# A graph-attention pair stage rebuilt: negated scores, another order of merges and multiplies, operands made earlier

## The chip, the cores and the metric

The kernel runs on one core of a Trainium2 chip. The time is the device time of one execution in microseconds (us), and lower is better. The engines are TensorE (PE in the profile, with PEld for its weight loads), VectorE (DVE), ScalarE (ACT), GpSimd (POOL) and SyncE (SP, which only issues transfers here). They run beside each other and meet at semaphores.

## The reference, cut to what matters

Two layers, each with a graph network, an attention-like mix and a small mixture of experts, on 625 nodes with 512 features and 10,000 edges. The change is in the second layer's graph network, a graph attention with 8 heads of 64, and in products around it:

```python
def _gat_forward(x, edge_index, W_e, W_r, a):          # x: 625 x 512
    h_e = einsum('nf,hfd->hnd', x, W_e)
    h_r = einsum('nf,hfd->hnd', x, W_r)
    a_src, a_dst, a_dif, a_abs, a_prd = split(a, 5, axis=1)
    diff = h_r[:, dst] - h_r[:, src]
    score = (s_src[src] + s_dst[dst] + diff . a_dif
             + |diff| . a_abs + (h_r[:, src] * h_r[:, dst]) . a_prd)
    alpha = leaky_relu(score, 0.2)
    att = softmax of alpha over the edges of one src
    out = segment_sum(att[:, :, None] * h_e[:, dst], src)
```

Beside it stand a linear attention with its projections (`L1_mix`) and, on either side, the two expert stages, whose first products have 512 + 96 columns.

## The kernel before, in words

The score of an edge depends on its two ends alone but for the term in `|diff|`. So the kernel does it in two stages.

**Edge turns** (40 of them, `TURNS`). The 10,000 edges are 80 columns of 125. In each turn two columns get their `|diff|` term: one from rows that GpSimd gathers from a table in HBM (L644, two gathers), one from one-hot products on TensorE (L896, L909). VectorE makes the scores (L1753 to L1767), and GpSimd scatters them, by column, into two tables of pairs in HBM (L654, `pairs[0]` and `pairs[1]`, each 625 x 625 x 8), whose other places hold -1e30. Beside this run the linear attention's products, a few per turn: `KEYS`, `QUERIES`, `VALUES`, `KEYS_TURNED`, `CONTEXT`, `ATTENDED`, `PROJECTED` (L91 to L97) say in which turn which product comes. They share two slots of PSUM.

**Operands.** After the last turn, TensorE turns the eight heads of `hrx` (L974 to L976, `("rT", h)`). ScalarE makes `rhsx` from each (L1266) and VectorE `lhsx` (L1815), after it has finished the small factors `prdx` and `not_last` (L1804 to L1811).

**Pair stage.** Five tiles of 125 source nodes, eight heads each: 40 pairs g = 8 i + h. For a tile, SyncE loads its rows of both tables, the first into one of two buffers `pt`, the second into `stage`, in two halves (L521 to L533). It waits for the buffer's old tile and, for a half of `stage`, for the four merges that read it. For one pair:

- TensorE makes the product of `lhsx` and `rhsx` (L988, by `product`, L694), 625 columns as 512 + 113.
- VectorE adds the table and takes the row's maximum (L1844), takes -0.2 of that (L1850), applies the leaky ReLU (L1851, both inputs the same SBUF tile), and makes the exponent's bias (L1854).
- ScalarE takes the exponential (L1283), GpSimd multiplies by the counts of edges (L674).
- TensorE transposes the result four pairs later (`LAG`; L993), ScalarE copies it (L1277), TensorE multiplies it with `hea` (L1003).
- VectorE merges the next tile's two tables with a maximum, a head's width at a time (L1830): two merges behind each of the heads 4 to 7, and all eight of the first tile before the first pair.
- After heads 3 and 7 of a tile, six pairs late, VectorE divides by the sums, adds to `x` (L1867 to L1875) and takes the statistics of the finished tile (L1310 to L1314), with GpSimd's power behind them (L573).

The slots of PSUM go round in an order written out in `psum_jobs` (L100); pair products and transposes share three. So TensorE's transposes for pair g - 4 take the slot that VectorE empties with L1844 of pair g - 1.

The two expert stages make their first products with the same `product`, 608 columns as 512 + 96 (L865, L1015).

## Time and profile before

| what | us |
|---|---|
| median of 3 runs | 1163.75 (1163.67 to 1176.94) |
| the profiled execution's own time | 1156.31 |
| its span, first to last instruction | 1154.5 |
| edge turns, first gather to last scatter landed | 695.6 to 919 |
| loads and merges of the first tile | 919 to 937.2 |
| pair stage, first L1844 to last L1851 | 937.2 to 1087.3 |
| rest: last sums, transposes, second expert stage, store | 1087.3 to 1154.5 |

The profile is that of one execution. A stretch's row gives the busy time of each engine and the clock that TensorE was granted as a share of full speed: 1.00 is 2.4 GHz and 0.50 is 1.2 GHz, and values between are a mean of the two. A timeline's row gives the start of an instruction (or of a run of like ones), its length, engine, line, operation and operands, and in brackets how long the engine had been idle and for whom. A busy TensorE is not one at its peak, since its matmuls are pipelined.

### The profile page before, as it was taken

What the parts mean: (1) busy time and instruction counts of PE and PEld (TensorE: products, weight loads), DVE (VectorE), ACT (ScalarE), POOL (GpSimd) and SP (SyncE); (2) the same over time, 40 slices, a digit from 0 to 9 for tenths busy, and PEclk for the clock granted to TensorE, in tenths of its full rate; (3) what the DMA queues carried; (4) which work ended last, traced back from release to release, by engine and by line L of the source; (5) the groups of instructions that cost most, each with busy time, mean ns of one, the idle gap of its engine ahead of it and who ended that gap; (6) DMA issues with size and microseconds to landing.
All of it is one profiled execution on the core that took longest, in us unless ns stands there. A gap on an engine that the chain in (4) does not pass through costs nothing.

```text
span 1154.5 us, 11895 instructions
## 1 busy us (share of the span) xinstructions
PE 1017.9 (88%) x4204; PEld 656.2 (57%) x4204; DVE 799.6 (69%) x1363; ACT 320.1 (28%) x561; POOL 361.5 (31%) x321
## 2 busy tenths in 40 slices
PE   7779988999999988999896988999879758888888
PEld 6755488644475445744443436666665436677744
DVE  8994496534587566954435378998988779998732
ACT  5682264311400123022103112221211214333401
POOL 5371700000020102001000117777777514444300
PEclk9889995999999998999897998999989759876999
DMA  9997020021410024001120324333333274442001
GB/s 295 310 310 232 0 100 1 1 90 39 151 37 0 1 90 132 5 0 53 45 109 0 136 49 139 102 98 93 101 95 96 89 311 179 178 176 89 9 1 45
DMA packets 65315, 115.09 MB, mean 100 GB/s; under 512 B 11393, under 2 KB 43393, under 8 KB 63341
## 3 DMA queue, kind: packets, MB, share of 16 engines
q1 hardware_dynamic: 56301, 93.08, 23.7%
q0 software_dynamic: 8960, 21.31, 6.7%
q8 instruction: 32, 0.52, 0.2%
q14 instruction: 22, 0.18, 0.0%
HBM read 85.88 MB, written 28.49 MB: 99 GB/s over the span
## 4 chain that ended last, share of the span: by engine, by line
PE 49%; DVE 24%; POOL 11%; issue 8%; DMA 6%; ACT 1%; DVEq 0%; POOLq 0%; SPq 0%
PE ps L699 25%; PE ps L826 8%; POOL arena L644 6%; DMA pairs<-arena,pairi 5%; PE ps L724 4%; PE ps L691 4%; DVE arena L1500 4%; POOL pairs L654 3%; DVE arena L1844 3%; DVE arena L1851 3%; PE ps L1003 2%; PE ps L876 2%; PE ps L1027 2%; PE ps L762 2%; DVE arena L1830 1%
## 5 line engine op out<-in xcount | busy, mean ns | idle before, releaser
L699 PE MATMUL ps<-arena 128*125 128x512 f32 (+4 forms) x576 | 250.4, 584 | 14.7 <-DVE small L1844 7.9
L699 PEld LDWEIGHTS ps<-arena 128*125 128x125 f32 (+2 forms) x576 | 112.5, 205 | 135.0 <-issue 121.5
L573 POOL TENSOR_TENSOR small<-small 125x1 f32<-125x1 f32 x50 | 33.0, 660 | 440.6 <-DVE small L1314 440.6
L699 PE MATMUL ps<-arena,xnT 128*125 128x512 f32 (+1 forms) x440 | 166.3, 536 | 1.6 <-DVE x L1743 1.6
L691 PE MATMUL ps<-ident,arena 125*128 125x125 f32 (+3 forms) x545 | 89.6, 310 | 57.3 <-DVE small L1844 17.9
L699 PEld LDWEIGHTS ps<-arena,xnT 128*125 128x125 f32 x440 | 76.5, 189 | 84.5 <-issue 83.7
L691 PEld LDWEIGHTS ps<-ident,arena 125*128 125x128 f32 (+3 forms) x545 | 74.8, 182 | 79.4 <-issue 30.5
L909 PE MATMUL ps<-ex_low,high 125*125 125x512 f32 x400 | 107.3, 416 | 0.0
L1185 ACT ACTIVATE arena<-ps,cols 128x125 f32<-128x125 f32 x120 | 43.2, 466 | 213.4 <-PE ps L691 213.4
L654 POOL DMA_INDIRECT pairs<-arena,pairi x80 | 87.6, 1095 | 26.1 <-issue 25.0
L674 POOL TENSOR_TENSOR arena<-arena,counts 125x625 f32<-125x625 f32 x40 | 62.7, 1567 | 102.5 <-ACT arena L1283 102.5
L909 PEld LDWEIGHTS ps<-ex_low,high 125*125 125x125 f32 x400 | 74.2, 194 | 16.7 <-issue 0.5
L724 PE MATMUL ps<-arena 125*125 125x314 f16 x400 | 66.6, 332 | 16.6 <-DVE arena L1357 15.6
L1039 ACT ACTIVATE arena<-ps 125x625 f32<-125x625 f32 (+4 forms) x79 | 49.3, 647 | 105.1 <-PE ps L691 102.1
L724 PEld LDWEIGHTS ps<-arena 125*125 125x125 f16 x400 | 59.9, 154 | 23.2 <-DVE arena L1357 18.8
L826 PE MATMUL ps<-arena 128*125 128x512 f32 x160 | 70.5, 593 | 1.7 <-DVE arena L1505 1.7
L1561 DVE TENSOR_TENSOR x<-x,ps 125x512 f32<-125x512 f32 x30 | 20.5, 685 | 61.1 <-PE ps L699 25.6
L1283 ACT ACTIVATE arena<-arena,small 125x625 f32<-125x625 f32 x40 | 32.7, 817 | 100.6 <-DVE small L1854 100.6
L1003 PE MATMUL ps<-arena 125*125 125x96 f32 x400 | 59.9, 307 | 0.0
L1003 PEld LDWEIGHTS ps<-arena 125*125 125x125 f32 x400 | 57.8, 226 | 0.0
L1767 DVE TENSOR_REDUCE arena<-arena 125x8 f32<-125x512 f32 x80 | 54.6, 683 | 2.2 <-DMA pairs<-arena,pairi 0.8
L1844 DVE CUSTOM_DVE_ANT_0 arena<-ps,arena 125x625 f32<-125x625 f32 x40 | 51.5, 1287 | 4.9 <-PE ps L699 4.8
(211 smaller groups left out, 1594.3 us busy)
## 6 DMA issues: line engine op xcount, KB each, us to landing
pairs<-fill SPq DMA_DIRECT2D x10, 2500.0 KB, 22.0
arena<-pairs SPq DMA_DIRECT2D x5, 2500.0 KB, 9.5
arena<-pairs SPq DMA_DIRECT2D x10, 1250.0 KB, 12.3
arena<-in_mw SPq DMA_DIRECT2D x6, 2048.0 KB, 8.3
arena<-in_rows SPq DMA_DIRECT2D x16, 250.0 KB
arena<-in_qkv_w SPq DMA_DIRECT2D x1, 3072.0 KB
arena<-in_cw SPq DMA_DIRECT2D x3, 1024.0 KB, 5.3
arena<-in_w_qkvT SPq DMA_DIRECT2D x1, 3072.0 KB
```

What stands on the lines that cost most here:

```text
L644: pool.indirect_dma_start(out=rows[:, g % GATHERS, :], out_offset=None, in_=table, in_offset=bass.IndirectOffsetOnAxis(ap=ends[:, 2 * g:2 ...
L654: pool.indirect_dma_start(out=pairs[n], out_offset=bass.IndirectOffsetOnAxis(ap=pairi[:, t:t + 1], axis=0), in_=sc[:, t % SCORES, :], in_o ...
L674: pool.tensor_tensor(S[:, h, :], S[:, h, :], counts[:, i, 0:N].bitcast(F32), ALU.mult).then_inc(sig("pair_weighted"), 1)
L691: last = pe.transpose(slot[0:n, at:at + rows], src, ident[0:rows, 0:rows])
L699: last = mm(slot[0:m, lo:hi], lhsT_of(k), rhs_of(k)[:, lo:hi], start=(k == 0), stop=(k == ks - 1))
L724: last = mm(ps[0:P, 512 * i:512 * i + HALF], one_hot[:, k, 0, P * i:P * (i + 1)], one_hot[:, k, 1, 0:HALF], start=False, stop=False, skip_ ...
L826: last = mm(slot[0:P, lo:lo + 512], nodes(hT, i)(k), w1[:, k, lo:lo + 512], start=(k == 0), stop=(k == KC - 1))
L909: last = mm(product_at[0:P, at:at + D], hotsT[e % 2][:, i, :], part[:, i, :], start=(part is hr_high and i == 0), stop=(part is hr_low and ...
L1003: last = mm(sums[0:P, at:at + WIDE], exTh[:, h, P * k:P * (k + 1)], hea[:, v0:v0 + WIDE], start=(k == 0), stop=(k == NT - 1), skip_group_c ...
L1039: return act.activation(dst, src, ACT.Copy)
L1767: v.tensor_reduce(sc[0:P, t % SCORES, :], src.rearrange("p (h e) -> p h e", h=H), AX_X, ALU.add)\
L1844: ring.emptied(v.tensor_tensor_reduce(S[:, h, :], slot[0:P, 0:N], p3[:, :, h], 1.0, -3e38, ALU.add, ALU.max, smax[:, 0, h:h + 1]), ("pair" ...
```

## The change

- **Negated scores.** L1844's operation takes the scale -1 and a minimum, so `S` holds negated scores. The bias is then one instruction, `min(0.2 low, low)`, and the leaky ReLU another, also with a minimum; L1850 is gone, and the bias comes first. The exponential has the scale -1.
- **Merge by head.** One merge behind every pair of the first four tiles, where there were two behind each of the heads 4 to 7.
- **Three table buffers.** `pt` has three, at 14300, 19300 and 5000. SyncE waits for the buffer of tile i - 3. The third overlaps `wo1` and the bias `b1or`, so its first load waits for the last `("y1", i)`. `S` keeps six pairs (`SCORED`) and `exTh` three (`TURNED`), where both kept eight.
- **GpSimd's multiply timed.** The multiply of pair g waits, beside the exponential, for the merge behind pair g + 1; in the last tile, for L1851 of pair g + 1.
- **Operands in the edge turns.** The turns of `hrx` come in turns 32 to 39, one head each, and ScalarE makes both `rhsx` and `lhsx`. `prdx` and `not_last` are made before the first edge turn. `PROJECTED` becomes turns 34, 36, 38 and two more behind the last, and the first tile's loads wait for `("oT", 3)` and no longer for `("y1", 4)`.
- **Halved products.** `halves_product` cuts 625 or 608 columns in the middle, across two banks of PSUM, for keys and queries, `oT`, the pair products and both expert stages.

```diff
-    jobs += [(("rT", h), "dve") for h in range(H)]
+    for e in range(PROJECTED[-1] + 1):
...
-        pt = [view(14300 + DT * n, DT) for n in range(2)]
+        pt = [view(at, DT) for at in (14300, 19300, 5000)]
...
-            ring.wait_emptied(sp, ("y1", NT - 1))
+            ring.wait_emptied(sp, ("oT", KC - 1))
             for i in range(NT):
-                if i >= 2:
-                    ring.wait_emptied(sp, ("pair", i - 2, H - 1))
+                if i == 2:
+                    ring.wait_emptied(sp, ("y1", NT - 1))
+                if i >= 3:
+                    ring.wait_emptied(sp, ("pair", i - 3, H - 1))
...
                     pool.wait_ge(sig("pair_exp"), g + 1)
-                    pool.tensor_tensor(S[:, h, :], S[:, h, :], counts[:, i, 0:N].bitcast(F32),
+                    if (g + 1) // H + 1 < NT:
+                        pool.wait_ge(sig("merged"), H + g + 2)
+                    elif g + 1 < NT * H:
+                        pool.wait_ge(sig("bias_ready"), g + 2)
+                    Sg = S[:, g % SCORED, :]
+                    pool.tensor_tensor(Sg, Sg, counts[:, i, 0:N].bitcast(F32),
                                        ALU.mult).then_inc(sig("pair_weighted"), 1)
...
+            def halves_product(slot, m, lhsT_of, rhs_of, ks, n):
+                at, cut = across_banks(n).start, n // 2
+                for lo, hi in ((0, cut), (cut, n)):
+                    for k in range(ks):
+                        last = mm(slot[0:m, at + lo:at + hi], lhsT_of(k), rhs_of(k)[:, lo:hi],
+                                  start=(k == 0), stop=(k == ks - 1))
+                return last
...
+            def rows_turned(h):
+                slot = ring.wait_filled(act, ("rT", h))
+                rows = slot[0:HX, 0:128 * NT].rearrange("p (i n) -> p i n", i=NT)[:, :, 0:P]
+                act.activation(rhsx[:, h, :].rearrange("p (i n) -> p i n", i=NT), rows,
+                               ACT.Identity, scale=not_last, bias=ident[0:HX, HX - 1:HX])
+                ring.emptied(act.activation(lhsx[:, h, :].rearrange("p (i n) -> p i n", i=NT),
+                                            rows, ACT.Identity, scale=prdx_of(0, h),
+                                            bias=prdx_of(1, h)), ("rT", h))
...
                     ring.emptied(v.tensor_tensor_reduce(
-                        S[:, h, :], slot[0:P, 0:N], p3[:, :, h], 1.0, -3e38, ALU.add, ALU.max,
-                        smax[:, 0, h:h + 1]), ("pair", i, h))
+                        Sg, slot[0:P, across_banks(N)], p3[:, :, h], -1.0, 3e38, ALU.add,
+                        ALU.min, smax[:, 0, h:h + 1]), ("pair", i, h))
...
-                    st.did(TS(smax[:, 2, h:h + 1], smax[:, 0, h:h + 1], -0.2, None, ALU.mult))
-                    st.did(STT(out=S[:, h, :], in0=S[:, h, :], scalar=0.2, in1=S[:, h, :],
-                               op0=ALU.mult, op1=ALU.max))
-                    st.wait()
-                    STT(out=smax[:, 1, h:h + 1], in0=smax[:, 0, h:h + 1], scalar=-1.0,
-                        in1=smax[:, 2, h:h + 1], op0=ALU.mult, op1=ALU.min)\
+                    low = smax[:, 0, h:h + 1]
+                    STT(out=smax[:, 1, h:h + 1], in0=low, scalar=0.2, in1=low, op0=ALU.mult,
+                        op1=ALU.min)
+                    STT(out=Sg, in0=Sg, scalar=0.2, in1=Sg, op0=ALU.mult, op1=ALU.min)\
                         .then_inc(sig("bias_ready"), 1)
-                    if i + 1 < NT and h >= 4:
-                        merge(i + 1, 2 * (h - 4))
-                        merge(i + 1, 2 * (h - 4) + 1)
+                    if i + 1 < NT:
+                        merge(i + 1, h)
```

## Rows read from the trace of the kernel before

**Rows 1.** Stretches: length, busy (count) PE, PEld, DVE, ACT, POOL; clock, DMA share, GB/s.

```profile
695.60:919.00 223.40, 201.04 (x911) 137.77 (x912) 193.65 (x316) 46.58 (x70) 172.11 (x160) 0.94 0.35 96
937.20:1087.50 150.30, 128.41 (x685) 102.61 (x686) 141.42 (x280) 53.53 (x75) 63.55 (x43) 0.78 0.36 142
```

**Rows 2.** Waits of GpSimd in the edge turns: us in total, times, longest.

```profile
POOL pairs L654 <- issue: 25.0, 79, 0.6
```

**Rows 3.** Groups by line in the pair stage: busy us, mean ns, idle before.

```profile
L674 POOL TENSOR_TENSOR arena<-arena,counts 125x625 f32<-125x625 f32 x39 | 61.4, 1574 | 100.7 <-ACT arena L1283 100.7
...
L1844 DVE CUSTOM_DVE_ANT_0 arena<-ps,arena 125x625 f32<-125x625 f32 x40 | 51.5, 1287 | 4.9 <-PE ps L699 4.8
L1851 DVE SCALAR_TENSOR_TENSOR arena<-arena 125x625 f32<-125x625 f32 x40 | 43.6, 1089 | 0.0
...
L1830 DVE TENSOR_TENSOR arena<-arena 125x625 f32<-125x625 f32 x33 | 25.2, 803 | 0.0
...
L1850 DVE TENSOR_SCALAR small<-small 125x1 f32<-125x1 f32 x40 | 6.1, 154 | 1.4
L1875 DVE TENSOR_TENSOR x<-x,arena 125x256 f32<-125x256 f32 x8 | 4.7, 591 | 0.3
```

**Rows 4.** Timeline (start, length) of one pair in which the two engines meet.

```profile
1006.65 1.29 POOL L674 TENSOR_TENSOR arena<-arena,counts 125x625 f32<-125x625 f32 x1 [1.87 <-ACT arena L1283]
...
1007.09 1.52 DVE L1851 SCALAR_TENSOR_TENSOR arena<-arena 125x625 f32<-125x625 f32 x1
```

**Rows 5.** Timeline of a pair with two merges ahead of it.

```profile
994.36 1.52 DVE L1830 TENSOR_TENSOR arena<-arena 125x625 f32<-125x625 f32 x2
...
995.37 1.66 POOL L674 TENSOR_TENSOR arena<-arena,counts 125x625 f32<-125x625 f32 x1 [2.08 <-ACT arena L1283]
995.91 1.30 DVE L1844 CUSTOM_DVE_ANT_0 arena<-ps,arena 125x625 f32<-125x625 f32 x1
...
997.33 0.80 DVE L1851 SCALAR_TENSOR_TENSOR arena<-arena 125x625 f32<-125x625 f32 x1
...
998.16 0.16 DVE L1854 SCALAR_TENSOR_TENSOR small<-small 125x1 f32<-125x1 f32 x1
```

**Rows 6.** Timeline, TensorE: transposes after a tile's end, and two later products.

```profile
989.73 1.38 PE L691 MATMUL ps<-ident,arena 125*125 125x125 f32 x5 [3.62 <-DVE small L1844]
...
995.12 1.28 PE L691 MATMUL ps<-ident,arena 125*125 125x125 f32 x5
...
1001.09 1.26 PE L699 MATMUL ps<-arena 66*125 66x512 f32 x4
...
1003.81 1.26 PE L699 MATMUL ps<-arena 66*125 66x512 f32 x4
```

**Rows 7.** Stretches of 5 us around that tile's end; columns as in rows 1.

```profile
985.00:990.00 5.00, 1.38 (x6) 0.75 (x5) 4.76 (x12) 0.55 (x1) 2.44 (x2) 0.83 0.00 0
990.00:995.00 5.00, 5.00 (x19) 3.96 (x19) 4.90 (x10) 1.93 (x3) 1.67 (x1) 0.50 0.22 54
```

**Rows 8.** Timeline: the queue of the loads, and the first merges.

```profile
919.09 18.42 SPq L440 DMA_DIRECT2D arena<-pairs  x6
...
931.25 5.90 DVE L1830 TENSOR_TENSOR arena<-arena 125x625 f32<-125x625 f32 x8 [5.79 <-DMA arena<-pairs]
```

**Rows 9.** Stretch of 5 us behind the second tile's loads.

```profile
945.00:950.00 5.00, 3.05 (x7) 1.45 (x6) 4.90 (x8) 1.55 (x3) 1.58 (x2) 0.50 0.01 4
```

**Rows 10.** Timeline: the first gather; first and last of the operands' small steps.

```profile
695.65 1.57 POOL L644 DMA_INDIRECT arena<-table,srci  x1 [5.73 <-DVEq L1713]
...
911.49 0.15 DVE L1805 TENSOR_TENSOR prdx<-prdx 64x8 f32<-64x8 f32 x1
...
912.20 0.15 DVE L1809 TENSOR_SCALAR small<-ident 66x1 f32<-66x1 f32 x1
```

**Rows 11.** Chain that ended last: the first products of the two expert stages.

```profile
588.05 21.52 PE ps L699 x80
...
1099.05 21.52 PE ps L699 x80
```

152 lines of the change are left out of this document (79 added, 73 removed).

## The prediction, before the changed kernel was seen

> **What bounds the kernel now.** I read the stretches first, to split the span. In the edge turns, 223 us, GpSimd is busy 172 us with 160 instructions [rows 1]. That is not full, but the view of its waits shows what fills the rest: before its scatters it stands 25.0 us in 79 pieces in which it waits for nothing, 0.3 us each [rows 2]. So the turns run at the pace at which GpSimd issues. VectorE (194 us) and TensorE have some room there. The pair stage, 150.3 us, is another matter: VectorE is busy 141.4 us, 94% of it, and TensorE has a mean clock of 0.78 [rows 1]. Between the two lie loads: they are issued at 919.09, the first merge waits for them until 931.25, and the eight merges take to 937.2 [rows 8].
>
> The groups by line then say what VectorE does in the pair stage [rows 3]: 40 each of L1844 at 1.29 us and L1851 at 1.09 us, the merges at 0.80, and small steps. The odd one is L1851. The timeline shows it at 0.80 us where it runs alone [rows 5], and at 1.52 us where GpSimd's multiply has begun 0.44 us ahead of it [rows 4]. The multiply then takes 1.29 us; where a merge is running as it begins, it takes 1.66 us [rows 5]. The one that comes second waits. L1844, which has one input in PSUM, is not lengthened by a multiply beside it (1.30 us in [rows 5], its mean is 1.29).
>
> **The change, part by part.** The sum goes by the profiled execution (1156.31 us, of which 1154.5 are its span). The median of three runs is 7.4 us longer, and I carry that difference over unchanged.
>
> *The timed multiply.* It now begins as the merge of the next pair ends, beside L1844 of the pair after that. L1851 begins 1.42 us after L1844 (995.91 to 997.33, [rows 5]) and the multiply alone takes 1.29 [rows 4], so it fits if it starts within 0.13 us. Then all L1851 take 0.80: 40 x (1.09 - 0.80) = -11.6 us [rows 3, 5]. Bounds: 0 (it slips and they meet again) and -11.6; No row shows how soon the release reaches GpSimd; I take -11.6, and the slip is a rival of its own below. The multiply comes later than now, but the transposes that need it come four pairs later and, as now, wait for a slot of L1844 three pairs on, so this stays hidden by some 3 us.
>
> The Trainium skill (SBUF — State Buffer, Who interferes with whom) says that VectorE and GpSimd share a pair of ports as an exclusive lock: an operation of VectorE with two SBUF inputs and a GpSimd operation that reads SBUF do not overlap, and the later one blocks to the end of the first. The trace agrees (1.52 against 0.80). By that rule the multiply does not vanish but meets other work, and this speaks against a part of the gain.
>
> That other work is L1875, which adds to `x` from two SBUF tiles behind the merge in two steps of each tile. Its mean is 0.59 us over 8 [rows 3]. Where the multiply starts just ahead of it, it could lose up to 0.4 each; between 0 and 3.2 I take +1.6 us.
>
> *Negated scores.* L1850 goes: 40 x 0.154 = 6.1 us busy [rows 3]. How much of it ran beside its neighbours no row tells, so the gain lies between 0 and 6.1; I take half, -3.1 us. The bias is ready after L1851 as before.
>
> *Merge by head.* The count of merges is the same and so is their price, 0.78 (two in 1.55, [rows 5]). What moves is the first need: the second tile's first merge comes 2.25 us (1.42 + 0.83, [rows 5]) behind 937.2, not after four pairs. Its half of `stage` is not there. The loads of two tiles, in the order of the queue, end at about 945: in the 5 us behind, the transfers are idle [rows 9]. From 919.1 to 945 that is 26 us for four equal pieces, 6.5 each, so the last half (3.2 us) begins near 942. VectorE waits from 939.5 to 942 or, with the landing, 943: +2.5 to 3.5, I take +3 us. From then on a step is 1.42 + 0.83 + 0.78 = 3.03 us, and the third buffer brings each tile's first table a tile earlier, so no later load is late.
>
> *TensorE as the next bound.* At full clock it needs 2.72 us for a pair (1001.09 to 1003.81, [rows 6]), at half clock 5.39 (989.73 to 995.12). The full clock suffices for 3.03, not for the last tile, which has no merges: 2.25 against 2.72 there, 7 steps, up to +3.3; part of that is given back in the blocks of sums, where VectorE is the later one. I take +2.5 us.
>
> At half clock TensorE is the bound of any step. After a tile's sums it stands idle 3.62 us [rows 6], its clock falls from full to half (0.83 as a mean of 5 us, then 0.50, [rows 7]), and VectorE pays: L1844 waits 4.8 us for products over the whole stage [rows 3]. With steps of 3.03 instead of twice that with two merges in every second half, a half-clock pair costs more (5.39 against 3.03). The idle gap itself gets some 0.8 us shorter, one merge less. Between no stalls (-4.8) and 29 us (below) I take +2 us, nearer to now because the pause that starts it is still there.
>
> *Operands in the edge turns.* The block between 911 and 925 vanishes, but it ran beside the last scatters and the loads, which set the merges' start [rows 8]; nothing is gained by it. In turns 34 to 38 TensorE had a projection in every turn and now has one in every second, with the turned rows beside. ScalarE takes on two operations a head, with 46.6 us busy of 223 [rows 1]. Both stay behind GpSimd's issue; if that cover were gone, eight turned heads would cost some 0.7 us each, 5.5 in all (five transposes take 1.38 at half clock, [rows 6]). The two late projections run while the loads do; the third buffer waits for them, and it is issued only after six others. But the small factors are now made ahead of the first gather, which waits for VectorE [rows 10]: from 911.49 to 912.35, 0.86 us. GpSimd's 160 instructions shift with it: +0.9 us.
>
> *Halved products.* Five products of 608 columns take 21.52 us in each expert stage, and that is the chain that ended last [rows 11], 4.30 each. The eight passes of 96 columns are the ones too short to cover a weight load. If one of 304 covers it no better, nothing is gained. At full clock a product is 16 passes of 304 columns at two cycles a column (an estimate: the pair products' 625 columns in four passes fit in their 1.26 us, [rows 6]), 16 x 0.253 = 4.05. So up to -0.25 each, 10 of them: 0 to -2.5, I take -2.1 us. In the pair stage and the turns it is hidden.
>
> **Sum.** -11.6 + 1.6 - 3.1 + 3 + 2.5 + 2 + 0.9 - 2.1 = -6.8 us, 1149.5 on the profiled execution's count. Against the median, 1163.75 - 6.8 = **1157 us**.
>
> **Rivals.** *The full gain.* The steadier rhythm keeps the clock up: TensorE's 2.72 of 3.03 leaves it 0.3 us of idle a step, where a step with two merges (1.42 + 0.83 + 1.55 = 3.80) left over 1. Then the 4.8 us of stalls go too (instead of +2), the last tile gives 2.5 less, and L1875 loses nothing: -6.8 - 6.8 - 2.5 - 1.6 = -17.7, **1146 us**. For it: in an even stretch the pairs ran at full clock [rows 6]. Against: the pause behind each tile remains. The Trainium skill (TensorE: Matmul & The Clock Gate, Part 1: The HAM clock gate) says that half rate is the default and activity lifts it; by that rule fewer and shorter pauses would bring this rival's time, and the trace shows both levels.
>
> *The multiply misses its window.* Only 0.13 us of margin; a later start of 0.3 us on every pair lets L1851 wait again. The 11.6 us stay: -6.8 + 11.6 = +4.8, **1168.6 us**. For it: the two engines start on semaphores of different ages. Against: two waits that have both long been met but one.
>
> *TensorE's low clock takes the stage* (the other side). A mean clock of 0.78 [rows 1] is 44% of 150 us at half rate, 66 us. If those all bind, each of the 12 pairs in them takes 5.39 and not 3.03: 12 x 2.36 = 29 us, 27 more than I put in: **1184 us**. It decides against the change from about four such pairs beyond mine (6.8 / 2.36 = 2.9). Against: a TensorE that is the bound is never idle, and after the fall at 990 with no idle time in 5 us [rows 7] its pairs were back at 2.72 by 1001 [rows 6].
>
> *Nothing moves:* gains and new waits cancel, 1160 to 1166. It is the forecast's upper part.
>
> **How the numbers follow.** Forecast, with its neighbours 1150 to 1165: 0.55. Full gain, 1143 to 1150: 0.18. Missed window, 1165 to 1171: 0.15. Low clock, over 1171: 0.10. Other: 0.02. The range 1146 to 1171 leaves out the low clock's case and the end of the full gain, about 2 in 10. Over 2%, about what a measurement of this kernel can tell from no change, is 23 us: faster would need 1140, which no sum here reaches (0.05); slower needs 1187, the end of the low clock's case (0.05). Within 2%: 0.90.
>
> **What would show it.** In the profile after: L1851 with a mean near 0.80 us (right) or over 1.0 (missed window); the multiply near 1.3 us, not 1.57; one wait of L1830 for a load near 943; the first L1844 at about 938; L1844's waits for TensorE near 7 us; 20.3 us for five expert products. The forecast fails if L1851 stays long, or if the clock of the pair stage leaves 0.78 by much in either direction.

## The result, and the profile after

| | before | after |
|---|---|---|
| median of 20 runs each, us | 1165.24 (1156.36 to 1176.94) | 1158.63 (1149.24 to 1166.44) |
| profiled execution, its span | 1156.31, 1154.5 | 1153.63, 1151.5 |
| pair stage, first add to last leaky ReLU | 937.18 to 1087.30 = 150.12 | 937.61 to 1083.86 = 146.25 |
| VectorE busy in it | 141.27 | 131.06 |

The ratio after to before is 0.9945, 95% interval 0.9923 to 0.9967: 6.4 us faster, where 6.8 were forecast (1157 us). The size is right. Much of the way to it is not, and the experiments show that more was left lying than was gained.

In the changed kernel the add with its row's extreme is L1873 (it was L1844), the bias L1880 (L1854), the leaky ReLU L1882 (L1851), the merge L1858 (L1830), the addition to `x` L1901 (L1875), GpSimd's multiply L692 (L674), the pair product L726. VectorE's groups by line in the pair stage (busy us, mean ns, idle before and its releaser), which answer [rows 3]:

```profile
L1873 DVE CUSTOM_DVE_ANT_0 arena<-ps,arena 125x625 f32<-125x625 f32 x40 | 51.5, 1288 | 8.4 <-PE ps L726 8.1
L1882 DVE SCALAR_TENSOR_TENSOR arena<-arena 125x625 f32<-125x625 f32 x40 | 32.0, 800 | 0.0
L1858 DVE TENSOR_TENSOR arena<-arena 125x625 f32<-125x625 f32 x32 | 25.6, 800 | 4.2 <-DMA arena<-pairs 4.2
L1880 DVE SCALAR_TENSOR_TENSOR small<-small 125x1 f32<-125x1 f32 x40 | 9.8, 244 | 1.4
L1901 DVE TENSOR_TENSOR x<-x,arena 125x256 f32<-125x256 f32 x8 | 8.6, 1077 | 0.3
```

The leaky ReLU is at 0.80 in every pair, as forecast. But the bias, an instruction of one column, went from 0.159 to 0.244, and the addition to `x` from 0.591 to 1.077 on average. The bias in the kernel before:

```profile
L1854 DVE SCALAR_TENSOR_TENSOR small<-small 125x1 f32<-125x1 f32 x39 | 6.2, 159 | 1.3
```

The timeline of VectorE and then of GpSimd shows the pair in which this happens (start, length):

```profile
946.80 0.80 DVE L1858 TENSOR_TENSOR arena<-arena 125x625 f32<-125x625 f32 x1
947.52 1.30 DVE L1873 CUSTOM_DVE_ANT_0 arena<-ps,arena 125x625 f32<-125x625 f32 x1
948.74 0.08 DVE L1873 DVE_READ_ACCUMULATOR2_ANT small<- 125x1 f32 x1
948.86 0.41 DVE L1880 SCALAR_TENSOR_TENSOR small<-small 125x1 f32<-125x1 f32 x1
949.19 0.80 DVE L1882 SCALAR_TENSOR_TENSOR arena<-arena 125x625 f32<-125x625 f32 x1
```

```profile
947.75 1.50 POOL L692 TENSOR_TENSOR arena<-arena,counts 125x625 f32<-125x625 f32 x1 [29.14 <-ACT arena L1317]
```

The multiply starts 0.22 us after the add (947.75 against 947.52), not within 0.13, and takes 1.50, not 1.29. It ends at 949.25. The bias begins at 948.86, reads two SBUF operands (the same column twice), and lasts until the multiply is over. The leaky ReLU behind it is free again.

The other half of the picture is TensorE's clock. Stretches of the changed kernel, columns as in [rows 1], first the whole stage, then three pieces around the sums of the second tile's first half:

```profile
937.61:1083.86 146.25, 123.98 (x682) 102.75 (x683) 131.06 (x239) 54.38 (x75) 59.51 (x42) 0.80 0.38 147
970.00:975.00 5.00, 3.47 (x22) 2.42 (x20) 4.86 (x10) 1.39 (x2) 2.12 (x2) 1.00 1.06 454
975.00:980.00 5.00, 4.66 (x19) 4.13 (x20) 4.64 (x10) 2.21 (x3) 1.43 (x2) 0.59 0.32 131
980.00:985.00 5.00, 5.00 (x29) 4.50 (x29) 3.50 (x6) 1.67 (x3) 2.72 (x2) 0.73 0.76 256
```

TensorE stands idle for 1.87 us up to 975.34, its clock falls from 1.00 to 0.59, and in the 5 us behind it TensorE is busy throughout while VectorE works 3.50 of 5. Outside the stage, the five products of an expert stage are the rows of the chain of work that ended last, which answer [rows 11]:

```profile
589.35 20.48 PE ps L726 x80
...
1096.20 20.48 PE ps L726 x80
```

### The profile page after: what moved, and what is told of

Its sections match the earlier page's. It is cut to its first block, busy times and chain, and to the rows that moved or that the text cites. A ratio compares the mean times of both kernels' runs of the same rounds, so it can differ in the third digit from the quotient of the medians.

```text
span 1151.5 us, 11896 instructions
## 1 busy us (share of the span) xinstructions
PE 1009.2 (88%) x4204; PEld 667.0 (58%) x4204; DVE 781.3 (68%) x1315; ACT 325.8 (28%) x569; POOL 358.7 (31%) x321
## 4 chain that ended last, share of the span: by engine, by line
PE 50%; DVE 23%; POOL 11%; issue 8%; DMA 7%; ACT 0%; DVEq 0%; SPq 0%; POOLq 0%
PE ps L717 21%; PE ps L853 8%; POOL arena L657 6%; PE ps L726 5%; DMA pairs<-arena,pairi 5%; PE ps L709 4%; DVE arena L1534 4%; POOL pairs L667 4%; DVE arena L1873 3%; PE ps L751 2%; PE ps L1029 2%; DMA arena<-pairs 2%; PE ps L903 2%; PE ps L1054 2%; PE ps L789 2%
## 5 line engine op out<-in xcount | busy, mean ns | idle before, releaser
L717 PE MATMUL ps<-arena 128*125 128x512 f32 x400 | 180.2, 606 | 0.0
L586 POOL TENSOR_TENSOR small<-small 125x1 f32<-125x1 f32 x50 | 35.5, 710 | 435.5 <-DVE small L1348 435.5
L709 PE MATMUL ps<-ident,arena 125*128 125x125 f32 (+3 forms) x545 | 85.2, 298 | 51.1 <-DVE small L1873 14.2
L717 PE MATMUL ps<-arena,xnT 128*125 128x512 f32 x280 | 126.0, 608 | 4.2 <-DVE x L1786 4.2
L717 PEld LDWEIGHTS ps<-arena 128*125 128x125 f32 x400 | 75.2, 193 | 89.9 <-issue 89.9
L667 POOL DMA_INDIRECT pairs<-arena,pairi x80 | 87.2, 1090 | 25.5 <-issue 25.5
L717 PEld LDWEIGHTS ps<-arena,xnT 128*125 128x125 f32 x280 | 53.6, 194 | 69.7 <-issue 69.3
L692 POOL TENSOR_TENSOR arena<-arena,counts 125x625 f32<-125x625 f32 x40 | 58.0, 1452 | 105.7 <-ACT arena L1317 92.0
L726 PE MATMUL ps<-arena 66*125 66x313 f32 (+3 forms) x176 | 65.1, 500 | 24.6 <-DVE small L1873 16.3
L853 PE MATMUL ps<-arena 128*125 128x512 f32 x160 | 70.5, 593 | 1.7 <-DVE arena L1539 1.7
L1595 DVE TENSOR_TENSOR x<-x,ps 125x512 f32<-125x512 f32 x30 | 20.5, 684 | 62.1 <-PE ps L717 25.4
L1873 DVE CUSTOM_DVE_ANT_0 arena<-ps,arena 125x625 f32<-125x625 f32 x40 | 51.5, 1288 | 8.4 <-PE ps L726 8.1
L726 PEld LDWEIGHTS ps<-arena 66*125 66x125 f32 (+1 forms) x176 | 35.3, 220 | 36.7 <-DVE small L1873 18.0
```

Source lines behind the costliest of these rows:

```text
L667: pool.indirect_dma_start(out=pairs[n], out_offset=bass.IndirectOffsetOnAxis(ap=pairi[:, t:t + 1], axis=0), in_=sc[:, t % SCORES, :], in_o ...
L692: pool.tensor_tensor(Sg, Sg, counts[:, i, 0:N].bitcast(F32), ALU.mult).then_inc(sig("pair_weighted"), 1)
L709: last = pe.transpose(slot[0:n, at:at + rows], src, ident[0:rows, 0:rows])
L717: last = mm(slot[0:m, lo:hi], lhsT_of(k), rhs_of(k)[:, lo:hi], start=(k == 0), stop=(k == ks - 1))
L726: last = mm(slot[0:m, at + lo:at + hi], lhsT_of(k), rhs_of(k)[:, lo:hi], start=(k == 0), stop=(k == ks - 1))
L853: last = mm(slot[0:P, lo:lo + 512], nodes(hT, i)(k), w1[:, k, lo:lo + 512], start=(k == 0), stop=(k == KC - 1))
```

## The experiments

The kernel before ran beside each on the same chip, and the ratio is to those runs. "Stage" is the profiled stretch from the first add to the last leaky ReLU.

| kernel | median us | ratio to before, 95% interval | stage | VectorE busy in it | adds' wait for TensorE | merges' wait for the load |
|---|---|---|---|---|---|---|
| before | 1165.24 | 1 | 150.12 | 141.27 | 4.8 | 0 |
| changed | 1158.63 | 0.9945 (0.9923 to 0.9967) | 146.25 | 131.06 | 8.1 | 4.2 |
| 1 no timed wait | 1161.04 | 0.9937 (0.9899 to 0.9975) | 151.52 | 134.61 | 9.9 | 4.3 |
| 2 released by `bias_ready` | 1154.88 | 0.9917 (0.9883 to 0.9952) | 144.18 | 128.38 | 8.8 | 4.3 |
| 3 operands late | 1160.74 | 0.9977 (0.9929 to 1.0025) | 150.15 | 130.54 | 12.9 | 3.9 |
| 4 before, timed multiply alone | 1156.41 | 0.9912 (0.9871 to 0.9953) | 153.87 | 136.40 | 13.4 | 0 |
| 5 gaps filled | 1150.75 | 0.9883 (0.9797 to 0.9969) | 143.01 | 131.12 | 4.8 | 4.1 |
| 6 merges later | 1154.93 | 0.9938 (0.9884 to 0.9991) | 143.14 | 130.63 | 9.5 | 0 |
| 7 no timed wait, bias of one tensor | 1159.74, one run | none | 154.23 | 133.98 | 13.3 | 4.2 |
| 8 = 2 + 5 + 6, and filled ahead, too late | 1164.16 | 0.9998 (0.9952 to 1.0044) | 160.47 | 131.42 | 26.2 | 0 |
| 9 = 5 + 6, more filling | 1148.26 | 0.9862 (0.9814 to 0.9910) | 137.57 | 131.10 | 3.7 | 0 |
| 10 = 9, filled ahead too | 1145.73 | 0.9843 (0.9799 to 0.9887) | 135.90 | 131.28 | 1.9 | 0 |
| 11 = 10 + 2 | 1152.28 | 0.9871 (0.9822 to 0.9919) | 150.49 | 132.43 | 15.0 | 0.3 |
| 12 = 10, `x` added from PSUM, fewer filling products | 1141.11 | 0.9807 (0.9778 to 0.9837) | 131.69 | 126.39 | 2.7 | 0 |

A profiled stage is one execution, and the adds' waits for TensorE differ by 5 us between kernels whose pair stage is the same (8.1 and 12.9 in the changed kernel and in 3). So I read an edit's worth from VectorE's busy time and from the wait it is about, and the whole from the intervals. None of the runs 1 to 6 is parted from the changed kernel by its interval; 9 to 12 are.

### 1. The timed wait left out

```diff
-                    if (g + 1) // H + 1 < NT:
-                        pool.wait_ge(sig("merged"), H + g + 2)
-                    elif g + 1 < NT * H:
-                        pool.wait_ge(sig("bias_ready"), g + 2)
```

> The changed kernel with GpSimd's timed wait left out: the multiply again starts as soon as its exponential is there. My theory, that the time of the start is what keeps the multiply off the leaky ReLU: L1878 (the leaky ReLU, 0.80 in the changed kernel) goes to 1.0 to 1.5 us in the steps where they meet, L1858's merges stay near 0.80, and the stage from the first add to the last leaky ReLU goes from 146.25 to 152 to 158 us, the time up by 6 to 11 us. Rival, that one merge to a head instead of two in every other head separates them by itself: the leaky ReLU stays under 0.9 us on average and the time moves by under 2 us.

Measured, VectorE's groups in the stage (L1878 is this kernel's leaky ReLU, L1876 its bias):

```profile
L1878 DVE SCALAR_TENSOR_TENSOR arena<-arena 125x625 f32<-125x625 f32 x40 | 32.0, 800 | 0.0
...
L1876 DVE SCALAR_TENSOR_TENSOR small<-small 125x1 f32<-125x1 f32 x40 | 14.5, 362 | 1.4
```

My theory falls in its main point: without the wait the leaky ReLU is at 0.80 in all 40 pairs. It is not the time of the multiply that keeps it free. The change also put the bias ahead of the leaky ReLU, and now the bias is the first instruction that meets the multiply: 0.16 where it is alone, up to 1.22 where it is held up, 14.5 us in all. What the timed wait is worth in this kernel is the bias's 14.5 - 9.8 = 4.7 us, or 3.5 us of VectorE's busy time (134.61 - 131.06), not 11.6. The rival is half right: the leaky ReLU stays under 0.9, and in this kernel the bias ahead of it takes the block. The stage, 151.52, was just short of what I expected, and 1.8 us of it are waits for TensorE (9.9 against 8.1); by time the two kernels can't be told apart.

### 7. The same with a bias that reads one tensor

```diff
-                    STT(out=smax[:, 1, h:h + 1], in0=low, scalar=0.2, in1=low, op0=ALU.mult,
-                        op1=ALU.min)
+                    TS(smax[:, 1, h:h + 1], low, 0.2, low, ALU.mult, ALU.min)
```

> The changed kernel without the timed wait, and with the small bias instruction written as one that reads a single tensor from SBUF (its factor and its second term come as the instruction's scalars). Without the wait and with the two-tensor form the bias took 0.362 us on average and the leaky ReLU 0.80. My theory, that the multiply blocks whichever two-tensor SBUF instruction comes first while it runs: the bias comes back to 0.15 to 0.17 and the leaky ReLU behind it takes the block, 0.95 to 1.05 on average. Rival, that every small SBUF instruction is slowed by the multiply: the bias stays above 0.30 and the leaky ReLU at 0.80.

Measured: the view of one line gives least, median and largest length in ns, for the bias and for the leaky ReLU.

```profile
L1876 DVE TENSOR_SCALAR small<-small x40: 211/214/216, 938.2 to 1089.5; 125x1 f32<-125x1 f32 x40
```

```profile
L1877 DVE SCALAR_TENSOR_TENSOR arena<-arena x40: 799/801/1707, 938.4 to 1089.7; 125x625 f32<-125x625 f32 x40
```

This settles it for the two instructions. A bias that reads one tensor has the same length in every pair, 0.21, with the multiply beside it (21 of the 40) or not; and the block goes to the next instruction with two SBUF tensors, the leaky ReLU, which is longer than 0.85 in 15 of the 40 pairs and has a mean of 0.920. I had put the bias at 0.15 to 0.17 (this form is simply longer than the other, 0.21 against 0.16) and the leaky ReLU's mean a little higher. There is one execution of this kernel, so its time says nothing.

### 4. The timed multiply alone, in the kernel before

```diff
+                    i1, h1 = divmod(g + 1, H)
+                    if i1 + 1 < NT and h1 >= 4:
+                        pool.wait_ge(sig("merged"), H * (i1 + 1) + 2 * (h1 - 4) + 2)
+                    elif i1 < NT:
+                        pool.wait_ge(sig("bias_ready"), g + 2)
                     pool.tensor_tensor(S[:, h, :], S[:, h, :], counts[:, i, 0:N].bitcast(F32),
```

> The kernel before with one part of the change alone: its multiply waits for the next step's merges, or where there are none for the next step's bias. My theory, that the timed start is the largest part: the leaky ReLU L1851 goes from a mean of 1.09 to 0.80 to 0.85, 10 to 11.6 us of VectorE's time, of which the two small instructions before it (0.15 and 0.16) may give back up to 0.5 us each in the half of the steps without merges, so that the time falls by 2 to 10 us. Rival, that without the merges spread over all heads no start is free: where a step has no merges the multiply still meets the leaky ReLU, its mean stays above 0.95, and the time falls by under 2 us or rises.

Measured in its stage (L1849 the add, L1856 the leaky ReLU, L1880 the addition to `x`):

```profile
L1849 DVE CUSTOM_DVE_ANT_0 arena<-ps,arena 125x625 f32<-125x625 f32 x40 | 51.6, 1291 | 13.5 <-PE ps L704 13.4
L1856 DVE SCALAR_TENSOR_TENSOR arena<-arena 125x625 f32<-125x625 f32 x40 | 33.8, 846 | 0.0
...
L1880 DVE TENSOR_TENSOR x<-x,arena 125x256 f32<-125x256 f32 x8 | 9.2, 1156 | 0.3
```

In the old order the timed wait does what the prediction said: the leaky ReLU goes from 43.6 to 33.8 us. Of these 9.8 us, 4.5 come back in the addition to `x` (4.7 to 9.2). The time falls by 0.5 to 1.3%, as much as with the whole rebuilt stage. The profiled execution itself was not a good one (1163.92 us): a stage of 153.87 with 13.4 us of waits for TensorE.

### 2. The multiply released by `bias_ready`

```diff
-                    if (g + 1) // H + 1 < NT:
-                        pool.wait_ge(sig("merged"), H + g + 2)
-                    elif g + 1 < NT * H:
+                    if g + 1 < NT * H:
                         pool.wait_ge(sig("bias_ready"), g + 2)
```

> The changed kernel with the multiply's wait for the next head's merge replaced by one for that head's bias everywhere: it is issued while the merge runs and should start where the merge ends, without a semaphore's way from VectorE (in the changed kernel it starts 0.22 us after the add). My theory, that its end at 1.5 to 1.7 us after the add is what lengthens the small bias instruction from 0.16 to 0.41: the bias instruction comes back to 0.16 to 0.20, VectorE's busy time in the stage falls from 131 to 123 to 127 us, and the stage from 146.25 to 140 to 144 us, less than VectorE's gain, since TensorE needs 2.72 us for a pair. Rival, that the bias instruction is longer for another reason (its two operands): it stays at 0.24 on average and nothing moves. A second rival: the multiply gets in ahead of the merge, whose mean then goes from 0.80 to over 1.2, and the stage is longer by 5 us or more.

The semaphore `bias_ready` is raised by the leaky ReLU, since the bias now comes ahead of it. So the multiply is released as the next head's leaky ReLU ends, about where the merge begins.

Measured (L1878 is the bias, L1880 the leaky ReLU, L1856 the merge, L1354 the normalised `x`), the groups and then one place in the timelines of VectorE and of GpSimd:

```profile
L1856 DVE TENSOR_TENSOR arena<-arena 125x625 f32<-125x625 f32 x32 | 25.7, 804 | 4.3 <-DMA arena<-pairs 4.3
...
L1878 DVE SCALAR_TENSOR_TENSOR small<-small 125x1 f32<-125x1 f32 x40 | 6.6, 166 | 1.4
L1354 DVE TENSOR_SCALAR xn<-x,small 125x512 f32<-125x512 f32 x3 | 3.8, 1265 | 0.0
```

```profile
1000.57 0.81 DVE L1856 TENSOR_TENSOR arena<-arena 125x625 f32<-125x625 f32 x1
1001.29 1.52 DVE L1354 TENSOR_SCALAR xn<-x,small 125x512 f32<-125x512 f32 x1
```

```profile
1000.80 1.73 POOL L690 TENSOR_TENSOR arena<-arena,counts 125x625 f32<-125x625 f32 x1 [1.56 <-DVE arena L1880]
```

My theory holds in its cause: the bias is back at 0.166, and the merges are not delayed. In size it fell short: VectorE loses 2.7 us of work (131.06 to 128.38, not to 127 or less), and the stage, 144.18, is just outside 140 to 144. The multiply is issued while the merge runs, and its record is longer for it (most are 1.71 to 1.96 us), but it is over 1.44 us after the add began (952.60 against 951.16), where the changed kernel's was over after 1.73 (949.25 against 947.52). The bias, which begins 1.34 us after the add in both, meets only the last 0.1 us of it. That the multiply waits for the merge's end and starts then is my reading of the lengths. The bias gives 3.2 us and the addition to `x` 1.7 (8.6 to 6.9), and the normalised `x` takes 2.2 back: its three take 1.52, 1.74 and 0.54 us in place of 0.54 each; the two long ones begin behind a multiply's start, the short one ahead of it (1060.08 against 1060.31). It reads one SBUF tensor only, so it is not the number of tensors alone that decides who is blocked. The gain in the stage, 2.1 us, is below what two profiles of one kernel differ by.

### 3. The operands turned late again

```diff
-ROWS_TURNED = (32, 33, 34, 35, 36, 37, 38, 39)
+ROWS_TURNED = (40, 41, 42, 43, 44, 45, 46, 47)
```

with the three loops over turns carried on to turn 47.

> The changed kernel with its eight operand turns put behind the last edge turns again (as in the kernel before, though ScalarE still makes both operands). My theory, that the loads of the first tile's tables set the start of the pair stage and the place of the operands is hidden: the first add starts within 0.5 us of where it did (937.61), the time moves by under 1.5 us. Rival, that the move gained something: the first add starts 2 us or more later against the first load's issue, and the time goes up by as much.

Measured: the first load is issued at 922.4 and the first add begins at 940.47, 18.1 us later; in the changed kernel 919.8 and 937.61, 17.8; before 919.09 and 937.18, 18.1. VectorE's busy time in the stage is the same (130.54). So the move of the operands is hidden, as forecast. The first add is 2.9 us later against the span's beginning: 0.9 of that is there at the first gather (698.04 against 697.17), 1.7 arise in the turns, which have less to do here, and 0.3 behind them; the stage is longer by waits for TensorE. None of this can be put down to the moved work. The medians (1160.74 and 1158.63) don't part.

### 5. TensorE's gaps filled

```diff
+                if i < NT and g % 4 == 3 and g >= 11:
+                    bank = 0 if g % 8 == 7 else 512
+                    for _ in range(12 if g % 8 == 7 else 4):
+                        mm(ring.psum[3][0:P, bank + HW:bank + 512], lhsx[:, h, 0:P], rhsx[:, h, 0:128],
+                           start=False, stop=False, skip_group_check=True)
```

The columns that these products write are read by nothing.

> The changed kernel with products whose result nobody reads (125x128, into unused columns of PSUM) put behind the pair product before TensorE's two gaps of each tile: 4 in the shorter gap (0.96 to 1.87 us in the changed kernel), 12 in the longer one (2.15 to 3.06 us). Nothing else moves. My theory, that the granted clock falls to 0.5 after these gaps and that the add's waits for TensorE (8.1 us in the changed kernel, 8.8 to 13.4 us in the runs around it, the same work each time) come from that: the granted clock stays at 1.0 from the second tile on, the add's wait for TensorE falls to 1 to 3 us, VectorE's busy time stays at 131, and the stage falls from 146.25 to 138 to 142 us. Rival, that TensorE's work of 2.72 us a pair is itself what the add waits for: the wait stays at 7 us or grows by the 3.5 us of work a tile that is added, and the stage is 146 us or longer.

Measured, stretches of this kernel (the stage, one gap with 4 products, one with 12), and then the changed kernel's at the gap with 12.

```profile
939.01:1082.02 143.01, 129.76 (x815) 110.80 (x816) 131.12 (x239) 53.92 (x75) 59.54 (x42) 0.87 0.39 150
970.00:975.00 5.00, 5.00 (x35) 4.14 (x35) 4.86 (x10) 2.47 (x4) 2.81 (x2) 1.00 1.03 442
975.00:980.00 5.00, 4.01 (x22) 3.67 (x21) 4.93 (x10) 1.39 (x2) 1.29 (x1) 0.69 0.55 235
980.00:985.00 5.00, 5.00 (x20) 4.43 (x19) 3.83 (x7) 2.32 (x3) 1.51 (x1) 0.50 0.61 204
...
1020.00:1025.00 5.00, 4.54 (x36) 4.08 (x36) 4.76 (x13) 0.71 (x2) 1.29 (x1) 1.00 0.00 0
1025.00:1030.00 5.00, 5.00 (x34) 3.84 (x32) 4.92 (x9) 2.79 (x4) 3.65 (x3) 1.00 0.15 24
```

```profile
1020.00:1025.00 5.00, 2.85 (x17) 2.58 (x18) 4.86 (x11) 1.39 (x2) 1.22 (x1) 0.87 0.00 0
1025.00:1030.00 5.00, 5.00 (x20) 4.37 (x19) 4.93 (x9) 2.33 (x3) 2.95 (x4) 0.50 0.46 148
```

VectorE has the same work (131.12), TensorE has more, and the stage is 3.2 us shorter. At 1020 to 1030, where the changed kernel's clock fell to 0.87 and 0.50, it stays at 1.00. It still fell behind the first gap, where 4 products left 0.99 us of idle time, and at 1035 to 1045 (0.83 and 0.82) around another gap with 4, which left 0.95. By time the four executions (1149.78 to 1152.19) are not parted from the changed kernel's twenty (1149.24 to 1166.44), but by the clock they are: its mean over a whole execution is 0.927 to 0.931 here and 0.907 to 0.922 there. The adds' wait went from 8.1 to 4.8, not to 1 to 3, and the stage stopped 1 us above what I had expected. The Trainium skill (TensorE: Matmul & The Clock Gate, Part 1: The HAM clock gate) says that the clock is at half rate by default and is lifted and held by activity. The trace agrees: with more work in the gaps the clock of the stage is 0.87 in place of 0.80.

### 6. The second tile's merges later

```diff
-                        merge(i + 1, h)
+                        for k in (MERGED_AT[h] if i == 0 else (h,)):
+                            merge(i + 1, k)
```

with `MERGED_AT = ((), (), (0,), (1,), (2,), (3,), (4, 5), (6, 7))`, and the multiply's wait counted to match.

> The changed kernel with the merges of the second tile put later among the first tile's heads (none at heads 0 and 1, one at 2 to 5, two at 6 and 7), since the second tile's load lands only 6 us after the first add. My theory, that the wait of 4.2 us for that load is the whole price of starting to merge at the first head: the wait goes to 0 to 0.5 us and the stage is shorter by 2 to 4 us, less than 4.2, because TensorE at half clock then sets the first tile's steps. Rival, that TensorE's clock takes all of it back: the add's wait for TensorE grows by 3 us or more and the stage stays within 1 us of 146.25.

Measured (L1878 the add, L1863 the merge):

```profile
L1878 DVE CUSTOM_DVE_ANT_0 arena<-ps,arena 125x625 f32<-125x625 f32 x40 | 51.5, 1287 | 9.9 <-PE ps L731 9.5
...
L1863 DVE TENSOR_TENSOR arena<-arena 125x625 f32<-125x625 f32 x32 | 25.5, 801 | 0.0
```

The load's wait is gone, as the theory said. The wait for TensorE is 1.4 us longer (9.5 against 8.1) and the stage 3.1 us shorter, both as expected, but from one execution each: between two executions this wait differs by more.

### 8 to 11. The parts together

Runs 9 and 10: the merges of 6 and the products of 5, now 8 in place of 4 in the shorter gap; 10 has 34 more behind the third pair product, while the first tables are loaded:

```diff
+                if g == 2:
+                    for _ in range(34):
+                        mm(ring.psum[3][0:P, 384:512], lhsx[:, h, 0:P], rhsx[:, h, 0:128],
+                           start=False, stop=False, skip_group_check=True)
```

> The changed kernel with the later merges of the second tile and the gap products, of which there are now 8 in place of 4 in the shorter gap, since in the run with 4 the clock fell once more behind that gap (0.69 and 0.50 from 975 to 990). My theory, that the two causes add: the load's wait goes (4.2 us), the add's wait for TensorE falls to 2 to 4 us behind the first tile and to 2 to 3 us in it, and the stage from 143.0 and 143.1 us with either alone to 137 to 140 us, the time to 1145 to 1149 us. Rival, that the low clock of the first tile takes back what the later merges give: the stage stays at 142 us or longer.

> As the run before it, with 34 more products behind the third pair product, in the 10 us in which TensorE waits for the first tables (in the earlier try they stood behind the fourth, which waits itself for the first add, and so ran into the first steps at half clock: 26.2 us of waits for TensorE). My theory, that the first tile's half clock comes from that wait: the granted clock is 1.0 from the first step on, the add's wait for TensorE is under 3 us in all, the stage 134 to 138 us, the time 1143 to 1147 us. Rival, that the clock falls all the same in the first tile, whose steps leave TensorE idle until the first sums: nothing is gained over the run before it.

Measured, stretches of 9 and then of 10 (the stage, the first tile's end, the rest):

```profile
943.25:1080.82 137.57, 129.85 (x847) 108.58 (x848) 131.10 (x239) 53.24 (x75) 59.54 (x42) 0.92 0.41 156
...
960.00:965.00 5.00, 5.00 (x21) 4.44 (x20) 3.62 (x6) 1.51 (x2) 1.57 (x2) 0.57 0.74 256
965.00:1080.00 115.00, 110.75 (x785) 94.41 (x784) 110.57 (x204) 45.67 (x65) 51.26 (x36) 1.00 0.34 125
```

```profile
930.00:935.00 5.00, 5.00 (x48) 5.00 (x47) 2.74 (x4) 0.00 (x0) 0.00 (x0) 1.00 1.06 447
940.00:945.00 5.00, 4.47 (x8) 2.32 (x8) 4.89 (x11) 1.63 (x2) 1.35 (x1) 0.50 1.00 414
...
960.00:1075.00 115.00, 109.67 (x776) 93.24 (x776) 110.93 (x205) 44.86 (x64) 51.92 (x37) 1.00 0.34 126
```

With both gaps filled the granted clock is 1.00 over 115 us, and the two edits together give more than the sum of their parts: the stage is 8.7 us shorter than the changed kernel's, where 3.2 and 3.1 came from either alone. My reading is that run 5's 4 products in the shorter gap were too few; the number of products alone was not tried. By time, 9 is 0.9 to 1.9% below before, and clear of the changed kernel (0.9814 to 0.9910 against 0.9923 to 0.9967). Filling ahead (10) lifts the clock to 1.00 at 930 to 935, but it is at 0.50 again when the first pairs run: TensorE stands idle 3.9 us up to 940.53. On the clock the rival is right; the wait fell from 3.7 to 1.9 all the same, and whether the 1.7 us of the stage are more than chance stays open (the intervals overlap).

Run 8 had 36 of these products behind the fourth pair product, which waits for the first add, together with the edits of 2, 5 and 6.

> The changed kernel with the multiply released by the next head's bias everywhere (as in the second run), the second tile's merges put later, the products that fill TensorE's gaps, and 36 more of them ahead of the first step, while the first tables are loaded. My theory, that what is left over the steps of 2.72 us is the bias held up (3 us), the load (4.2) and the low clock (8): VectorE's busy time in the stage is 126 to 129 us, its waits for TensorE and the load under 6 us together, the stage 130 to 137 us, and the time 1142 to 1150 us. Rival, that TensorE's own work becomes the bound as soon as VectorE's steps are shorter: the waits for TensorE come back to 8 us or more and the stage is 138 us or longer.

Its timeline of TensorE shows what became of them:

```profile
937.39 2.45 PE L725 MATMUL ps<-arena 66*125 66x312 f32 x4 [10.40 <-DVE small L1881]
939.63 15.57 PE L1022 MATMUL ps<-arena 66*125 66x128 f32 x72
```

They ran in the first steps instead of ahead of them, at half clock, 15.57 us, and held the pair products up. That is my error in placing them. The merges are longer too (28.2 us against 25.5 in run 6), from the cause that run 11 shows.

Run 11 is 10 with the release of 2.

> As the run before it, with the multiply released by the next head's bias everywhere, so that it starts with the merge's end. My theory, that VectorE's steps get shorter by the 0.08 us on average that the small bias instruction loses (3 us in the stage), and that TensorE's 2.72 us take at least half of that back: the stage is shorter by 0 to 1.5 us. Rival, that the multiply gets in ahead of merges now and then (one merge took 2.1 us in the earlier run of all three): the stage is longer by 1 us or more.

In the profiled execution the stage is longer by 14.6 us, and the rival names the place. That execution, 1158.32 us, is a long one; the medians differ by 6.6 us, and the intervals overlap. Where the first tile has two merges behind one another, the multiply gets in between them. The timelines of VectorE and of GpSimd (L1866 the merge, L691 the multiply):

```profile
965.02 2.84 DVE L1866 TENSOR_TENSOR arena<-arena 125x625 f32<-125x625 f32 x2
```

```profile
965.25 1.94 POOL L691 TENSOR_TENSOR arena<-arena,counts 125x625 f32<-125x625 f32 x1 [2.93 <-DVE arena L1890]
```

Two merges that take 1.52 without it [rows 5] took 2.84. TensorE stood idle 2.05 us up to 969.31, the clock was at 0.56 and then 0.50 from 970 to 990, and the adds' waits rose from 1.9 to 15.0 us. The merges are longer by 4.0 us in all (29.4 against 25.4); the other 13.1 us are waits for TensorE. That these follow from the pause and the clock is likely by the order in time, and not shown by a run of its own. Releasing the multiply by the merges in those two heads alone was not tried.

### 12. The addition to `x` from PSUM

```diff
-                    TT(o.rearrange("p (h e) -> p h e", h=4), s4[:, :, 0:HD],
-                       r.unsqueeze(2).to_broadcast([P, 4, HD]), ALU.mult)\
-                        .then_inc(sig("sums_used"), 1)
-                    v.wait_ge(sig("sums_used"), 2 * j + b + 1)
-                    st.did(TT(x[:, j, 256 * b:256 * (b + 1)], x[:, j, 256 * b:256 * (b + 1)], o,
-                              ALU.add))
+                    for q in range(4):
+                        xq = x[:, j, 256 * b + HD * q:256 * b + HD * (q + 1)]
+                        last = STT(out=xq, in0=s4[:, q, 0:HD], scalar=r[:, q:q + 1], in1=xq,
+                                   op0=ALU.mult, op1=ALU.add)
```

> The kernel with the later merges, the gap products (here 5 and 9 in the two gaps, which get shorter) and the 34 products ahead, with the addition to x written otherwise: four instructions that read one quarter of the sums from PSUM, scale it and add x, in place of a scaling to SBUF (0.424 us) and an addition of two SBUF tensors (0.591 us on average in the kernel before, 1.075 in the run without this edit, eight of each). My theory, that the addition is long because it is blocked by the multiply, and that an instruction with one SBUF tensor is not: four instructions of 0.10 to 0.20 us each, 0.4 to 0.8 us in place of 1.50, so that VectorE's busy time in the stage falls by 5 to 8 us from 131.28 and the stage from 135.9 to 130 to 133 us. Rival, that the quarters cost as much as they save or are blocked as well (over 0.3 us each): the stage stays at 135 us or longer. A second rival, that TensorE is the bound by now: VectorE's busy time falls by 5 us or more, its waits for TensorE rise from 1.9 to 5 us or more, and the stage stays above 134 us.

The products in the gaps are fewer than in 10 as well (5 and 9 in place of 8 and 12), so the time is that of both edits; VectorE's busy time is that of the one shown.

Measured: one line's least, median and largest length in ns, then the stage.

```profile
L1914 DVE SCALAR_TENSOR_TENSOR x<-ps,small,x x40: 274/275/285, 972.1 to 1080.3; 125x64 f32<-125x64 f32 x40
```

```profile
940.19:1071.88 131.69, 123.77 (x794) 102.61 (x795) 126.39 (x255) 53.49 (x75) 59.65 (x42) 0.92 0.42 161
```

This instruction, with one of its two tensors in PSUM, has one length, 0.275, beside the multiply or not; each was longer than I had put it, but four in a row take 0.86 (at 985.38) in place of 0.424 + 1.075. VectorE loses 4.9 us of work, just short of the 5 to 8 expected, the stage 4.2 us, waits for TensorE stay small (2.7). This is the fastest of the kernels: 1141.11 us, 1.6 to 2.2% below before and, by ratio to before, 1.4% below the changed kernel (0.9807 / 0.9945).

## Why the prediction was right, step by step

The sum came to -6.8 us and the measurement to -6.4. Its terms, against the two profiled executions:

| term | forecast | measured | from |
|---|---|---|---|
| leaky ReLU to 0.80 | -11.6 | -11.6 | 43.6 to 32.0 |
| (not in the sum) bias held up | 0 | +3.4 | 40 x (0.244 - 0.159) |
| addition to `x` meets the multiply | +1.6 (0 to 3.2) | +3.9 | 4.7 to 8.6 |
| L1850 gone | -3.1 (-6.1 to 0) | -6.1 | whole of its 6.1 |
| second tile's load late | +3 (2.5 to 3.5) | +4.2 | wait at 943.97 |
| TensorE as the bound, low clock | +4.5 | +3.3 | waits 4.8 to 8.1 |
| small factors ahead of the first gather | +0.9 | +1.3 | below |
| halved expert products | -2.1 | -2.1 | 2 x (21.52 - 20.48) |

**The timed multiply: right in size, wrong in cause.** I took all 11.6 us as the wait's work and wrote that the bias follows the leaky ReLU "as before". The diff puts the bias first, and with two SBUF operands it became the instruction that the multiply blocks. Run 1 shows the leaky ReLU free without the wait, run 7 shows that of the bias and the leaky ReLU the first with two SBUF tensors is blocked, run 4 that the wait alone is worth 9.8 us of the leaky ReLU in the old order. Without the wait the meeting costs 8.1 us at the bias (run 1, 40 x (0.362 - 0.159)) or 4.8 us at the leaky ReLU (run 7, 40 x (0.920 - 0.800)), where it cost 11.6 before. So part of the 11.6 went with the rest of the new order, and which edit took it no run shows. The gap of 1.42 us into which the multiply should fit is there (947.52 to 948.86 is 1.34), the start and the length were underrated: 0.22 and 1.50 us. The rival of the missed window had the lateness nearly right (0.3 us on every pair) and the victim wrong: the price is 0.085 us on the mean bias, up to 0.27 where they meet, not the 11.6 us of the leaky ReLU.

The Trainium skill (SBUF — State Buffer, Who interferes with whom), from which the prediction took the block, also says that an instruction of VectorE with at most one SBUF input, outside the modes in which it uses both ports, does not contend. For the small instructions the trace agrees on both sides: 0.21 and 0.275 us in all 40 places with one SBUF tensor (runs 7 and 12), 0.16 to 0.43 with two in the changed kernel. The condition on the modes matters: the normalised `x`, with one SBUF tensor and 512 columns, took 1.52 and 1.74 us where the multiply had begun before it, and 0.54 where it began first (run 2); that it ran in such a mode no trace shows. The prediction applied the rule to the long instructions alone, and it holds for one of a single column.

**The addition to `x`: undersized.** I worked from its mean of 0.591, and that mean mixed two things: in the trace of before, five of the eight take 0.42 and three 0.87. After, three take 0.94 and five 1.15 or 1.16. So each can lose 0.73, not 0.4, and all eight lose something, where I counted on half. In run 4, which times the multiply in the old order, all eight take 1.15 to 1.17: a multiply that always starts behind a merge always stands ahead of this instruction.

**L1850: undersized.** Half of its 6.1 us was a hedge between 0 and all; all of it went from VectorE's busy time. With it went 1.3 us of idle time: the two small instructions before had 1.4 and 1.3 us ahead of them in all, the one after has 1.4.

**Load, TensorE and clock.** The wait came at 943.97 (I wrote near 943) and took 4.2 us; in run 6 the stage is 3.1 us shorter without it. The waits for TensorE are 8.1 us where I wrote near 7. But the range of this term was the thing to look at: in six kernels with the pair stage of the changed one or nearly so (the changed one, 1, 2, 3, 6, 7) the same wait was 8.1 to 13.3 us. Filling the gaps brought it to 4.8 (run 5), with the later merges to 3.7 (9) and with the filling ahead to 1.9 (10). I had named the pause behind each tile as its start and left it there as given.

**Operands, first gather, halves.** Run 3 shows the operands' move hidden. The first gather is at 697.17 instead of 695.65, 1.52 later; 1.30 of that is there at the first expert stage already (589.35 against 588.05), ahead of everything that was changed, and 0.22 are left. With the 1.04 us that the halved products save in between, the shift to set against the forecast's 0.9 is about 1.3 (0.53 of it the small factors' own stretch, 694.75 to 695.28; where the rest is from I did not follow). The halves are right to 0.1 us. Behind the stage 0.6 us were lost (12.34 from the last leaky ReLU to the second expert stage, against 11.75).

**The sum.** The terms as measured make -3.7 us, and the two profiled executions differ by 2.7 (1156.31 and 1153.63), the medians by 6.6. Stretch by stretch the two spans differ by +1.3 us ahead of the first expert stage, -1.0 in it, +1.3 from there to the first gather, -0.8 in the edge turns, -0.3 from the first load to the first add, -3.9 in the pair stage, +0.6 behind it, -1.0 in the second expert stage and +0.9 after that, -3.0 in all. The sum had a term for four of these nine; the other five, which it put at nothing, moved by 0.3 to 1.3 us, and no run shows why. The profiled execution of before was also a lucky one: it is as short as the shortest of the twenty (1156.36). The mechanisms were mostly the right ones, but that -6.8 met -6.4 so closely is in part luck: three terms were off by 2.3 to 3.4 us with both signs, and one profiled execution stands for the median only to within the waits for TensorE. In the changed kernel the five executions with a mean clock under 0.915 took 1162.0 to 1166.4 us, the eight with 0.918 or more 1149.2 to 1159.2. The full gain of 1146 us, which I gave 0.18 as an accident of the rhythm, is about what runs 9 and 10 reach on purpose (1148.3 and 1145.7 us), by way of the clock and the load and without the part in the addition to `x`, which still loses 3.9 us there.

## What to carry to other kernels

Before a wait is used to move one engine's work out of another's way, list the instructions behind it by what they read, the small ones too: here the block went to the first of them with two SBUF tensors, and an operand left in PSUM (run 12) or a form that reads one tensor (run 7) took a small instruction out of the list. A long one with a single SBUF tensor was blocked all the same (the normalised `x` in run 2). Where a profile shows the granted clock falling behind a regular pause of TensorE, fill the pause before anything else is trimmed: work that nobody reads made this stage shorter, and where TensorE kept its clock a trimmed VectorE showed nearly in full (run 12: 4.9 us of work, 4.2 of the stage). And judge each edit by the busy time and the wait that it touches, since the waits for the clock differ from one execution to the next by as much as a whole edit is worth.

## What was not expected of the hardware

- A multiply of GpSimd that runs 0.39 us into an instruction on one column of 125 rows lengthens that from 0.16 to 0.41; held up from the start it took up to 1.22.
- A pause of 1.87 us in TensorE's work was followed by a granted clock of 0.59, one of 2.05 us by 0.56 and then 0.50 for 15 us. Of two of about 1 us, one was followed by 0.69 and 0.50 (0.99, run 5) and one by 1.00 (1.05 up to 964.80, run 10). In runs 9, 10 and 12 gaps of up to 0.66 us between 965 and the stage's end left it at 1.00. But in run 6 one of 2.36 us, up to 1054.00, was followed by 1.00 for 20 us, so the length of a pause alone does not say whether the clock falls.
- A multiply released while a merge runs was over 0.3 us earlier, counted from the add, than one released by the merge's semaphore (run 2, 1.44 against 1.73). Between two merges in a row it takes its turn (run 11).
- The normalised `x`, an instruction with one SBUF tensor of 512 columns, took 1.52 and 1.74 us where the multiply had begun before it, and 0.54 where it began first (run 2).
